# Moving four parts of batch 2's query/key projection in the prologue of an attention + sparse-FFN kernel

## The reference

```python
q, k = rope(x @ Wq.T), rope(x @ Wk.T); v = x @ Wv.T
attn = softmax(where(causal, q @ k.T / 4, -inf))
x = layernorm(x + (attn @ v) @ Wo.T)
h = silu(x @ w_gate) * (x @ w_up)          # keep the 2 largest |h| of every 4
x = layernorm(x + sparsify_2to4(h) @ w_down)
```

## Time and profile before

| | |
|---|---|
| median of three timed executions | 729.64 us |
| the profiled execution, its own time | 727.83 us |
| its span (first to last instruction) | 726.1 us |
| mean granted TensorE clock over the span | 0.974 of full |
| busy share TensorE / VectorE / ScalarE / GpSimd | 92% / 77% / 56% / 44% |

### The profile page before, as it was taken

How to read it: one execution, slowest core, us unless ns; L and a number is a source line. 1 busy time by engine, 2 the same in 40 slices (tenths; PEclk the granted TensorE clock), 3 DMA queues, 4 the chain that set the end, 5 groups by cost and what they waited for, 6 DMA issues and landing times. The chain is left out here.

```text
span 726.1 us, 13794 instructions
## 1 busy us (share of the span) xinstructions
PE 665.6 (92%) x5264; PEld 492.8 (68%) x5264; DVE 561.0 (77%) x825; ACT 407.6 (56%) x578; POOL 320.0 (44%) x317
## 2 busy tenths in 40 slices
PE   7979788999999999998989988989999999999984
PEld 6655554657565565655645656788989898989883
DVE  5888656778777787877787376878897989898976
ACT  5551566576867768666576764535453535363522
POOL 4485876677867778532233133024040312213030
PEclk9997899999999999999999999989999999999997
DMA  4048646355464554558111102112111102010101
GB/s 127 29 107 164 156 111 188 115 149 159 135 180 146 150 168 125 155 155 285 39 59 34 59 1 78 40 45 72 59 36 51 58 29 81 5 58 0 59 1 58
DMA packets 48815, 67.61 MB, mean 93 GB/s; under 512 B 6456, under 2 KB 27448, under 8 KB 48760
## 3 DMA queue, kind: packets, MB, share of 16 engines
q1 hardware_dynamic: 47860, 65.23, 31.1%
q10 hardware_dynamic: 900, 1.64, 0.9%
HBM read 43.12 MB, written 23.07 MB: 91 GB/s over the span
## 5 line engine op out<-in xcount | busy, mean ns | idle before, releaser
L941 DVE TENSOR_REDUCE bmax<-mx_ps 128x8 f32<-128x1024 f32 (+1 forms) x148 | 180.8, 1222 | 80.8 <-PE mx_ps L1219 79.9
L782 ACT ACTIVATE prob<-ex_ps 128x1024 f32<-128x1024 f32 x160 | 163.9, 1024 | 84.6 <-PE ex_ps L1249 80.3
L612 POOL TENSOR_SCALAR_AFFINE_SELECT prob<-prob 128x512 f32<-128x512 f32 x128 | 88.2, 704 | 128.3 <-ACT prob L782 128.3
L1266 PE MATMUL pv_ps<-prob,v_sb 128*32 128x512 f32 (+3 forms) x1024 | 83.1, 443 | 2.0 <-POOL prob L612 2.0
L1204 PEld LDWEIGHTS mx_ps<-mask_b,half_id 64*128 64x128 bf16 x592 | 16.9, 94 | 80.3 <-DVE bmax L941 68.8
L1204 PE MATMUL mx_ps<-mask_b,half_id 64*128 64x128 bf16 x592 | 46.0, 234 | 24.6 <-DVE bmax L941 21.9
L1507 POOL TENSOR_TENSOR hm_l<-v_sb,hm_h 128x2048 fp32r<-128x2048 f32 x4 | 18.5, 4622 | 90.4 <-ACT hm_h L1568 90.4
L1507 POOL TENSOR_TENSOR k_st<-v_sb,q_st 128x2048 fp32r<-128x2048 f32 x3 | 13.9, 4626 | 75.6 <-ACT q_st L1568 75.6
L1266 PEld LDWEIGHTS pv_ps<-prob,v_sb 128*32 128x32 f32 x1024 | 25.7, 110 | 28.9 <-issue 24.8
L1554 ACT ACTIVATE g_sb<-ex_ps 128x512 f32<-128x512 f32 x28 | 16.6, 591 | 45.7 <-PE ex_ps L1770 45.7
L1816 PE MATMUL mi_ps<-wd_h,q_st 128*128 128x256 f32 x128 | 37.7, 294 | 3.4 <-DVE k_st L1686 3.4
(11 more groups left out here) (261 smaller groups left out, 1987.2 us busy)
## 6 DMA issues: line engine op xcount, KB each, us to landing
y_sb<-x SPq DMA_DIRECT2D x12, 512.0 KB, 3.9
xT_sb<-xT SPq DMA_DIRECT2D x8, 512.0 KB, 4.4
q_st<-q_parts SPq DMA_DIRECT2D x32, 128.0 KB, 2.8
k_st<-k_parts SPq DMA_DIRECT2D x32, 128.0 KB, 3.0
x<-y_sb SPq DMA_DIRECT2D x8, 512.0 KB, 3.3
xh<-x SPq DMA_DIRECT2D x8, 512.0 KB, 3.9
q_parts<-qk_rot SPq DMA_DIRECT2D x14, 256.0 KB, 3.1
k_parts<-qk_rot SPq DMA_DIRECT2D x14, 256.0 KB, 2.8
```

What stands on the lines that cost most here:

```text
L612: nc.gpsimd.affine_select(out=block, in_=block, compare_op=ALU.is_ge, fill=0.0, base=0, pattern=[[0, n], [1, P]], channel_multiplier=-1).t ...
L782: nc.scalar.activation(out, ex_ps[:], ACT.Exp).then_inc(ex_act, 1)
L941: nc.vector.tensor_reduce(out=out, in_=src, axis=AX.X, op=ALU.max).then_inc(mx_read, 1)
L1266: last = nc.tensor.matmul(pv_ps[32 * g:32 * g + 32, P * kt:], v_sb[b % 2][:, kt, G4 * j + g, :], probs(g), start=kt == 0, stop=kt == 2, sk ...
```

## The change

Only the order of `PROLOGUE` is changed. Before: fills 14 to 19 of batch 0, QK(2,0), nm, fill 0 of batch 1, QK(2,1), fills 1 and 2, QK(2,2), fills 3 and 4, QK(2,3). After: fills 14 and 15 of batch 0, QK(2,0), fills 16 and 17, QK(2,1), fills 18 and 19, nm, fills 0 and 1 of batch 1, QK(2,2), fills 2 and 3, QK(2,3), fill 4. No instruction is added or removed; `nm`, QK(2,1) and the maxima's place in the rotation of the `mi_ps` tiles change places with each other.

```diff
-    ("F", 0, 13), ("R", 0, 15), *[("F", 0, f) for f in range(14, FILLS)], ("QK", 2, 0), ("nm", 0, 0),
-    ("F", 1, 0), ("QK", 2, 1), ("F", 1, 1), ("F", 1, 2), ("QK", 2, 2), ("F", 1, 3), ("F", 1, 4), ("QK", 2, 3),
+    ("F", 0, 13), ("R", 0, 15), ("F", 0, 14), ("F", 0, 15), ("QK", 2, 0), ("F", 0, 16), ("F", 0, 17), ("QK", 2, 1),
+    ("F", 0, 18), ("F", 0, 19), ("nm", 0, 0), ("F", 1, 0), ("F", 1, 1), ("QK", 2, 2), ("F", 1, 2), ("F", 1, 3),
+    ("QK", 2, 3), ("F", 1, 4),
```

## The result

The changed kernel takes 732.73 us (median of 22 executions, 728.11 to 735.85), the kernel before 729.42 us (22 executions on the same chips, 725.13 to 732.56). The ratio is 1.0038 [1.0023, 1.0053]: **slower, by 2.8 us**; the medians themselves are 3.3 us apart. That is at the upper edge of the range, 732.3: 729.42 and 2.8 make 732.2, and the median itself is 0.4 us above the edge. The likeliest case, no change that can be measured, did not come; rival 1 comes nearest.

What follows compares the result with a forecast made beforehand. VectorE was taken as the bound late in batch 0's fills, later the fill-and-reduction round through one buffer. Losses of 3.1 to 4.1 us less 1.97 and 1.1, taken as 0.5, on 729.64 gave 730.1 us, range 728.0 to 732.3.

Steps and rivals of the forecast that it cites:

- The likeliest case: Whole kernel: a change within 0.2%, or 1.5 us, which a measurement can't tell from none; chance 0.56.
- rival 1: Slower: QK(2,0), QK(2,1) and step 4's value quarters at half clock, +2.1 to +3.1 us, forecast 732.3; chance 0.27.
- Fill 16: Batch 0 prologue: VectorE stalls 2.4 us for this fill behind QK(2,0), which takes 2.7 us at half clock.
- QK(2,1): Prologue, between fills 17 and 18: clock up again, so fill 18's reduction costs VectorE only 0.45 us more.
- The maxima: End of batch 0: nmax 2.75 us late, low part 1.75 after it, fill 0 of batch 1 2.1 late; clock falls again.
- Fill 4 of batch 1: Prologue, behind QK(2,3): 3.1 us late, or 2.1 with the clock up all through.
- GpSimd: Rotation 0 near 59.8, rotation 7 at 74.05, masks free at 81.2, 0.7 earlier; value products no longer wait for it.
- The value quarters of step 4: TensorE, step 4: full clock once the idle stretch is gone, 2.64 us becomes 1.5, 1.1 us back.
- Step 5: Net shift reached at this step: 0.1 to 1.0 us late, taken as 0.5.
- the sum: Prologue to step 4: 3.1 to 4.1 us lost, less 1.97 and 1.1, taken as 0.5 and added to the median.
- Beyond step 5: Remaining steps, paced by fill and reduction through one buffer: the shift is carried to the end unchanged, within a microsecond.

Runs made afterwards that it cites:

- the three profiles: The changed kernel, no edit, profiled in three separate runs; medians 732.73 us, then 732.51 and 734.91 us in the repeats.
- the filled kernels: TensorE's gaps filled with extra matmuls whose results are overwritten: 725.15 us on the changed kernel, 728.75 us on the kernel before.
- the second half alone: Kernel before with only QK(2,2) and QK(2,3) each one fill earlier: 729.69 us, ratio 1.000.
- the first half alone: Kernel before with only QK(2,0) and QK(2,1) moved between batch 0's last fills: 731.24 us against 728.54, ratio 1.0037.
- the best kernel: Kernel before with overwritten matmuls in TensorE's gaps and GpSimd's first mask ahead of rotations 9 to 11: 722.90 us against 728.22.
- the changed one filled: Changed kernel with overwritten matmuls in TensorE's gaps, in the prologue and in steps 0 and 1: 725.15 us against 728.54, ratio 0.9952.
- before filled: Kernel before with the same overwritten matmuls, except the 8 ahead of nm: 728.75 us, ratio 1.0012.
- after with the mask first: Changed kernel with GpSimd's first mask ahead of rotations 9 to 11 of batch 2: 732.00 us against 729.21, ratio 1.0042.
- after filled in the prologue and in the steps: Two runs, changed kernel with overwritten matmuls in the prologue only, 727.77 us, or in steps 0 and 1 only, 726.59 us, against 729.21.
- before with the mask first: Kernel before with GpSimd's first mask ahead of rotations 9 to 11 of batch 2: 725.95 us against 728.22, ratio 0.9970.

## Why the prediction was right or wrong

- **Fill 16, right.** 2.4 us of stall predicted, 2.64, 2.65 and 2.16 found in the three profiles. QK(2,0) took 2.86 us for my 2.7.
- **QK(2,1), the step that failed.** "Then the clock should be up, a dense part lying behind it." It was up in the first profile (61.55 to 63.16; stall 0.27 against 0.45) and in the third, not in the second (stall 2.19). And what the first profile escaped at QK(2,1), the third met at QK(2,3). One execution of before showed the clock rise in one place, and I made of that the behaviour of all executions. Over many executions the changed kernel has more half clock than the one before: 13 of 22 at 0.965 or less, one of 81 before (none of the 29 in the table).
- **The maxima, right.** 2.7 us late (2.75 predicted) at `nmax`, low part 1.75 us behind it as worked out, fill 0 of batch 1 2.1 late. The fall of the clock behind the 2.46 us wait came as taken: QK(2,2) in 2.80 us. The Trainium skill (TensorE: Matmul & The Clock Gate, "Why this matters for your kernels") warns that idle gaps between bursts cost the clock. The trace agrees in direction, with 0.50 at 68 to 70 us, though this gap is shorter than those that the page warns of.
- **Fill 4 of batch 1, right for the first profile.** 3.0 late for 3.1; 6.4 and 5.5 in the others.
- **GpSimd, right but for the mask.** Rotation 7 at 74.85, which less 0.98 is 73.9 (74.05 predicted); the first mask at 81.22, less 0.98 80.2, 1.0 earlier than the 81.2 predicted, mostly because rotations 8 and 10, 1.61 and 1.73 us before, took 1.28 and 1.27. It changed nothing, as the products waited for no mask. No wait of the products is left; they start 1.8 us late (85.49 less 0.98, against 82.74; 1.2 to 2.1 predicted).
- **The value quarters of step 4, right.** 1.62 us for 1.5, at granted clock 1.00.
- **Step 5.** 0.4 us late in the first profile, inside the predicted 0.1 to 1.0. In the other two 4.0 and 3.0, the +2.1 to +3.1 of rival 1 and somewhat more. Rival 1 had QK(2,0) and QK(2,1) low, which came in the second only; in the third it was QK(2,0), QK(2,2) and QK(2,3). It also had step 4's quarters low, which came in none of the three.
- **From one execution to the median.** I added the sum to the median of all executions, as if each would meet the same clock. In executions at a clock of 0.972 or more the difference is 0.65 us, close to the 0.5 that I forecast, though from 4 executions. That fewer executions are of that kind is less than half of the measured difference; the rest is that the executions of the changed kernel in the low group are 3.0 us slower than those of the kernel before. Stalls at half clock under the moved parts are shown in three profiles, and the filled kernels show that keeping the clock up ends the loss; that they explain the other executions is argued, as only their mean clock is known.
- **Beyond step 5, the other step that failed.** I wrote that a shift at step 5 is carried to the end unchanged, and that the prediction is wrong if the two differ by over a microsecond. They do: from step 5 to the last fill (376 us) the three profiles of after lose another 2.7, 2.2 and 2.9 us, more than the 0.4 of the first one at step 5. The first and third lose 1.3 near 125 us and 1.4 to 1.6 near 370; the second loses nothing near 125, 1.5 near 345 and 0.8 near 370, and gets 2.2 back behind its last fill. The kernel before loses nothing in either profile. But the second half alone, equal to before in its median, shows 2.8 as well, the first half alone 2.7 and the best kernel 2.7. So those stretches can't be put to the moved parts.

  The part near 125 us goes with the clock in all 14 profiles. Busy times from 115 to 135 us, of the kernel before, the changed one and the changed one filled:

```profile
115.00:135.00 20.00, 17.67 (x173) 11.20 (x171) 11.80 (x13) 11.95 (x17) 13.12 (x13) 0.91 0.60 174
```

```profile
115.00:135.00 20.00, 17.72 (x155) 11.27 (x152) 11.64 (x13) 11.91 (x16) 10.79 (x13) 0.83 0.57 166
```

```profile
115.00:135.00 20.00, 17.04 (x194) 11.28 (x196) 14.07 (x18) 12.61 (x18) 14.46 (x13) 1.00 0.56 161
```

  Four profiles have 0.91 there (before twice, after the second time, before filled) and keep their distance. Eight have 0.83 and lose 1.1 to 1.4 us: after twice, both halves, after with the mask first, after filled in the prologue and in the steps, and before filled with the mask first. Two have 1.00 and gain 1.4 to 1.5 us: after filled, and before with the mask first. What makes an execution meet one or the other isn't settled.

## What to carry to other kernels

Put filling work of TensorE where the engine that sets the pace waits in any case; between fills that feed a VectorE without slack each part costs what it takes beyond the slack, and at half clock the part itself grows: 2.86 us instead of 1.61, and a stall of 2.64 instead of 0.65 in this kernel. If the aim is to end a wait, first see whether the late engine's own queue can be reordered: three rotations behind one mask gave 0.3% where moving four parts cost 0.4%. Where a stretch sits at the edge of the clock's rise, take several profiles, count from an instruction ahead of the change, and compare the granted clocks of all executions before a sum from one is put on the median.

## What the runs showed of the hardware that was not expected

**One program, several clocks.** The same kernel, always on one core, took from 728.11 to 735.85 us, and the times go with the mean granted clock (0.974 to 0.960). The kernel before took from 726.31 to 733.01 us in 29 executions (0.974 to 0.967). The same projection part, QK(2,1), took 1.61 and 1.60 us in two executions and 2.85 in the third.

**A busy TensorE can stay at the lower level.** From 60 to 64 us of the second execution after, TensorE ran fills 16 and 17 and most of QK(2,1) and is recorded as busy throughout (2.00 of 2.00 in both stretches shown), at a granted clock of 0.50. A high busy share in the profile does not tell that the clock is up.

**Rotations beside another engine's work.** GpSimd's rotation instructions of 128x512 took 1.28 us in most places and 1.74 us behind the early mask (79.19). The mask is not the reason: in the kernel before two of them took 1.61 and 1.73 us (76.11, 78.92). All three overlap in time with an instruction of VectorE on the same tile `qk_rot` (75.85, 77.75; 78.65 with the mask first), which took 0.73, 1.75 and 1.14 us where two later ones of the kernel before took 0.68. What the two engines share there was not tried.
